# First keys' moves ahead of the small rows, the small rows on other queues, and a third score bank in the gaps of the job plan

## The reference

```python
# x: 2048 x 256; ctx_1024: 1601 x 256; E = 16 features in each of 16 heads
qh, kh, vh = heads(layernorm(x) @ Wq.T + bq), heads(ctx @ Wk.T + bk), heads(ctx @ Wv.T + bv)
scores = einsum('blhe,bshe->bhls', qh, kh) * tau + delta[:, None, None, :]
x = x + (softmax(scores / sqrt(E)) @ vh) @ Wo.T + bo
x = x + top1_expert(layernorm(x))           # 8 experts, weighted by the router's largest probability
x = x + windowed_attention(layernorm(x))    # tanh(cat @ W_c.T)
x = x + slot_mixture(layernorm(x))          # top 8 of 64 slots, GRU, slot attention, write back
```

## Time and profile before

| | us |
|---|---|
| median of 3 runs | 1069.53 (1069.47 to 1071.1) |
| the profiled execution | 1072.81, its span 1070.8 |
| PE busy / DVE busy / ACT busy in the span | 980.2 / 742.4 / 572.9 |
| maximum stage, first unit to first `pv` | 36.4 to 94.1 |
| round 0, rounds 1, 2, 3 begin at | 89.6, 249.8, 487.6, 725.6 |
| last score ends | 950.4 |

### The profile page before, as it was taken

How to read it: one execution, slowest core, us unless ns; L and a number is a source line. 1 busy time by engine, 2 the same in 40 slices (tenths; PEclk the granted TensorE clock), 3 DMA queues, 4 the chain that set the end, 5 groups by cost and what they waited for, 6 DMA issues and landing times.

```text
span 1070.8 us, 13621 instructions
## 1 busy us (share of the span) xinstructions
PE 980.2 (92%) x4794; PEld 389.6 (36%) x4794; DVE 742.4 (69%) x1704; ACT 572.9 (54%) x1063; POOL 64.5 (6%) x91
## 2 busy tenths in 40 slices
PE   7699999999899999889899989889899989889886
PEld 3353322233333334323333334323333334234643
DVE  5589888887777777767677687777677774126633
ACT  3366666666455456656455456656455466740330
POOL 3351000000000000000000000000000000100000
PEclk9899999999999999989899999999899899899899
DMA  7946500001000000001000000001000000040032
GB/s 190 190 88 112 123 1 16 16 2 35 1 16 1 15 1 11 6 1 55 1 16 1 16 1 13 4 1 55 1 16 1 1 1 21 21 127 1 1 98 79
DMA packets 34411, 36.19 MB, mean 34 GB/s; under 512 B 6766, under 2 KB 31387, under 8 KB 34083
## 3 DMA queue, kind: packets, MB, share of 16 engines
q1 hardware_dynamic: 33102, 34.43, 13.1%
q10 hardware_dynamic: 1162, 0.64, 0.4%
q0 software_dynamic: 80, 0.26, 0.1%
HBM read 21.55 MB, written 7.35 MB: 27 GB/s over the span
## 4 chain that ended last, share of the span: by engine, by line
issue 48%; PE 31%; DVE 8%; DMA 4%; SPq 3%; ACT 2%; POOL 2%; DVEq 1%; POOLq 0%; ACTq 0%
PE ps_o L1168 8%; PE ps_m L1084 8%; PE ps_e L1370 5%; DVE mx L1671 4%; DMA xres<-in_x 1%; PE ps_e L1041 1%; PE ps_m L1370 1%; SPq L558 1%; DMA q_stack<-probs 1%; PE ps_m L1188 1%; DMA d_parts<-delta_parts 1%; PE ps_m L1318 1%; POOL rstd L701 1%; POOL xres L753 1%; ACT probs L867 1%
## 5 line engine op out<-in xcount | busy, mean ns | idle before, releaser
L1671 DVE TENSOR_REDUCE mx<-ps_m 128x1 f32<-128x401 f32 x1024 | 536.1, 568 | 186.0 <-PE ps_m L1084 177.4
L867 ACT ACTIVATE probs<-ps_e 128x512 f32<-128x512 f32 (+1 forms) x763 | 438.3, 598 | 325.1 <-PE ps_e L1370 323.2
L1084 PE MATMUL ps_m<-k_stack,q_stack 99*128 99x401 bf16 x1024 | 318.6, 343 | 36.5 <-DVE mx L1671 27.0
L1370 PE MATMUL ps_e<-q_stack,k_stack 101*128 101x512 bf16 (+1 forms) x763 | 298.6, 393 | 11.2 <-ACT probs L867 9.4
L1168 PE MATMUL ps_o<-probs,v_heads 128*32 128x512 f32 (+1 forms) x1664 | 232.2, 632 | 0.0
L1370 PEld LDWEIGHTS ps_e<-q_stack,k_stack 101*128 101x128 bf16 (+1 forms) x763 | 75.5, 100 | 264.6 <-ACT probs L867 172.4
L1084 PEld LDWEIGHTS ps_m<-k_stack,q_stack 99*128 99x128 bf16 x1024 | 101.6, 99 | 183.0 <-DVE mx L1671 123.5
L1272 PE MATMUL ps_m<-expert_w,xnT 128*128 128x512 f32 x192 | 98.4, 593 | 0.7 <-DVE xb L1809 0.7
L1168 PEld LDWEIGHTS ps_o<-probs,v_heads 128*32 128x32 f32 (+1 forms) x1664 | 33.4, 109 | 62.7 <-issue 49.8
L867 ACT ACTIVATE probs<-ps_m 128x512 f32<-128x512 f32 (+1 forms) x69 | 41.5, 601 | 15.6 <-PE ps_m L1370 15.6
L1809 DVE SCALAR_TENSOR_TENSOR xb<-ps_m,hot,xb 128x256 f32<-128x256 f32 x84 | 40.6, 483 | 7.8
(11 more groups left out here) (333 smaller groups left out, 730.7 us busy)
## 6 DMA issues: line engine op xcount, KB each, us to landing
q_stack<-q_parts SPq DMA_DIRECT2D x78, 64.0 KB, 2.6
expert_w<-in_expert_wT SPq DMA_DIRECT2D x2, 1024.0 KB, 12.9
xres<-in_x SPq DMA_DIRECT2D x4, 512.0 KB, 3.8
x<-xres SPq DMA_DIRECT2D x4, 512.0 KB, 3.0
probs<-x SPq DMA_DIRECT2D x1, 2048.0 KB, 8.7
k_stack<-alphaT SPq DMA_DIRECT2D x10, 200.1 KB, 7.7
probs<-in_ctxT SPq DMA_DIRECT2D x3, 512.0 KB, 8.1
q_parts<-probs SPq DMA_DIRECT2D x4, 384.0 KB, 2.5
```

Source lines behind the costliest of these rows:

```text
L867: act.activation(probs[0:n, k % 2, h, :], score_bank(c, k, h)[0:n, :], ACT.Exp).then_inc(s["exp_done"], 1)
L1084: pe.matmul(ring_bank((n1, u))[:, 0:SPLIT], qst[0:MAX_ROW, g, h, P * t:P * t + P], kst[0:MAX_ROW, HG * g + h, QUARTER_START[q]:QUARTER_STA ...
L1370: pe.matmul(score_bank(c, k, h)[0:n, :], kst[0:ROWS, HG * g + h, P * st:P * st + n], qst[0:ROWS, g, h, :], start=True, stop=True).then_inc ...
L1671: dve.tensor_reduce(mx[:, q, col:col + 1], ring_bank((n1, u))[:, 0:SPLIT], AX.X, ALU.max)\
```

## The change

Queues first. `k_soft` is a new list of four semaphores; the last move of delta's rows, the ones and four key moves go to POOL's queue, the store of delta's parts to ACT's, and "U" leaves `START` for unit 8.

```diff
-GATHER_SP = ((0, 4, 2, 1, 5, 3), (0, 4, 2, 1), (0, 4, 2))
-GATHER_ACT = ((), (5, 3), (1, 5, 3))
+GATHER_SP = ((0, 4, 2, 1), (0, 4, 2, 1), (0, 4, 2))
+GATHER_POOL = ((5, 3), (5, 3))
+GATHER_ACT = (1, 5, 3)
...
-START = [("D",), ("L", 0), ("C",), ("K", 0, 0), ("N", 0), ("S",), ("K", 1, 0), ("T", 0), ("Q", 0, 0), ("G", 1), ("K", 2, 0), ("g",),
-         ("K", 3, 0), ("V", 0), ("V", 1), ("G", 2)]
-START += [("V", i) for i in range(2, V_EARLY)] + [("L", 1), ("U",)]
-
-BESIDE = []
+START = [("D",), ("L", 0), ("C",), ("K", 0, 0), ("N", 0), ("S",), ("K", 1, 0), ("T", 0), ("Q", 0, 0), ("K", 2, 0), ("g",),
+         ("K", 3, 0), ("V", 0), ("V", 1), ("G",)]
+START += [("V", i) for i in range(2, V_EARLY)] + [("L", 1)]
+
+BESIDE = [(8, ("U",))]
...
@@ sync
-            sp.wait_ge(s["consts_set"], 1)
-            sp.dma_start(kst[MAX_ROW:MAX_ROW + 2, 0:3 * HG, :], ones_sb[0:2, 0:S].unsqueeze(1).broadcast_to((2, 3 * HG, S)))\
-              .then_inc(s["ld_k"], 16)
-            sp.dma_start(qst[DELTA_ROW:DELTA_ROW + 3, :, :, :].rearrange("p g h t -> p g (h t)"),
-                         ones_sb[0:3, :].unsqueeze(1).broadcast_to((3, NG, HG * CT))).then_inc(s["ld_ones"], 16)
-            sp.wait_ge(s["delta_parts"], 1)
-            sp.dma_start(d_parts.rearrange("a (p s) -> p a s", s=P), delta3[:]).then_inc(s["delta_stored"], 16)
-            sp.wait_ge(s["delta_stored"], 16)
-            sp.dma_start(kst[DELTA_ROW:DELTA_ROW + 3, 0:3 * HG, :], d_parts[:, 0:S].unsqueeze(1).broadcast_to((3, 3 * HG, S)))\
-              .then_inc(s["ld_delta_k"], 16)
...
@@ gpsimd
             pool.memset(ones_sb, 1.0).then_inc(s["consts_set"], 1)
+            pool.wait_ge(s["consts_set"], 1)
+            pool.dma_start(qst[DELTA_ROW:DELTA_ROW + 3, :, :, :].rearrange("p g h t -> p g (h t)"),
+                           ones_sb[0:3, :].unsqueeze(1).broadcast_to((3, NG, HG * CT))).then_inc(s["ld_ones"], 16)
...
             pool.memset(eb[:], 0.0).then_inc(s["fills_set"], 1)
+            pool.wait_ge(s["delta_stored"], 16)
+            pool.dma_start(kst[DELTA_ROW:DELTA_ROW + 3, 0:3 * HG, :], d_parts[:, 0:S].unsqueeze(1).broadcast_to((3, 3 * HG, S)))\
+                .then_inc(s["ld_delta_k"], 16)
+            for i, rows in enumerate(GATHER_POOL):
+                first_col, end_col, last_block = KEY_PIECES[i]
+                pool.wait_ge(s["blk_parts"], BLOCK[last_block] + 1)
+                for j, row in enumerate(rows):
+                    move_k(pool, 0, (row,), k_soft[len(rows) * i + j], first_col, end_col)
             scale_shift(1)
...
                 if step[0] == "L":
                     scale_shift(step[1])
+                if step == ("L", 2):
+                    pool.dma_start(kst[MAX_ROW:MAX_ROW + 2, 0:3 * HG, :],
+                                   ones_sb[0:2, 0:S].unsqueeze(1).broadcast_to((2, 3 * HG, S))).then_inc(s["ld_k"], 16)
...
@@ scalar, step "D"
+                    act.wait_ge(s["delta_parts"], 1)
+                    act.dma_start(d_parts.rearrange("a (p s) -> p a s", s=P), delta3[:]).then_inc(s["delta_stored"], 16)
```

```diff
+def score_plan():
+    hold = {name: h for name, _, _, h in JOBS}
+    jobs = [(HG * SLOTS * (c + 1) + AT[name], name, c) for name, c in JOB if JOB[name, c][0] == 1]
+    plan, last, last_score = [], [None] * 3, {}
+    for n in range(HG * SLOTS * NC):
+        near = any(at <= n + 2 and n < at + hold[name] + 2 for at, name, _ in jobs)
+        b = min(range(2 if near else 3), key=lambda i: -1 if last[i] is None else last[i])
+        begun = [(name, c) for at, name, c in jobs if at < n]
+        plan.append((b, last[b], begun[-1] if begun else None))
+        last[b] = n
+        last_score.update({(name, c): last[2] for at, name, c in jobs if at == n})
+    return plan, last_score
...
             need(eng, bank_taken[b], n)
+            if b and LAST_SCORE[job, c] is not None:
+                eng.wait_ge(s["exp_done"], LAST_SCORE[job, c] + 1)
...
-            return ps_e[h % 2] if c else (*ps_e, ps_x)[(HG * k + h + 1) % 3]
+            return (*ps_e, ps_x)[SCORES[HG * (SLOTS * c + k) + h][0]]
...
-                        need(pe, s["exp_done"], HG * SLOTS * c + HG * k + h - (1 if c else 2))
+                        b, last, job = SCORES[HG * (SLOTS * c + k) + h]
+                        if last is not None:
+                            pe.wait_ge(s["exp_done"], last + 1)
+                        if b == 2 and job:
+                            wait_taken(pe, *job)
```

More of the change, by code:

```diff
@@ L204 @@
 RING_NO = ring_numbers()
+def score_plan():
[10 more added lines that the diff above has]
+    return plan, last_score
+SCORES, LAST_SCORE = score_plan()
 HALF_JOBS = (["ot", "y", "t1", "router", "e0", "e1", "gateT"] + [f"e{i}" for i in range(2, NE // 2)]
@@ L401, in build @@
         k_half = [sem(f"k_half{i}") for i in range(2)]
+        k_soft = [sem(f"k_soft{i}") for i in range(4)]
         q_loaded = [sem(f"q_loaded{g}") for g in range(NG)]
@@ L528, in block_cols, with wait_first_keys @@
             return k_cols[BLOCKS[b][1]][1] if BLOCKS[b][0] == "K" else CT
+        def wait_first_keys(eng, half):
+            if half == 0:
+                eng.wait_ge(k_half[0], 16 * sum(len(rows) for rows in GATHER_SP[:2]))
+                for moved in k_soft:
+                    eng.wait_ge(moved, 16)
+            else:
+                eng.wait_ge(k_half[1], 16 * K_PARTS)
         def k_loads(g):
@@ L628, in _ @@
                 sp.wait_ge(q_stored[m], 16 * NC)
-            for i, half in enumerate(k_half):
-                sp.wait_ge(half, 16 * K_PARTS * HALF_OF_PIECE.count(i))
+            for i in range(2):
+                wait_first_keys(sp, i)
             sp.wait_ge(k_loaded[1], 16 * K_PARTS)
@@ L634, in _ @@
             sp.wait_ge(s["ld_k"], 16)
+            sp.wait_ge(s["ld_ones"], 16)
             sp.wait_ge(s["ld_delta_k"], 16)
@@ L826, in step @@
                     act.activation(delta_a[:], delta_a[:], ACT.Identity, scale=E ** -0.5).then_inc(s["delta_hi"], 1)
+                    act.wait_ge(s["delta_parts"], 1)
+                    act.dma_start(d_parts.rearrange("a (p s) -> p a s", s=P), delta3[:]).then_inc(s["delta_stored"], 16)
                 if kind == "G":
-                    i = args[0]
-                    first_col, end_col, last_block = KEY_PIECES[i]
+                    first_col, end_col, last_block = KEY_PIECES[2]
                     act.wait_ge(s["blk_parts"], BLOCK[last_block] + 1)
-                    move_k(act, 0, GATHER_ACT[i], k_half[HALF_OF_PIECE[i]], first_col, end_col)
+                    move_k(act, 0, GATHER_ACT, k_half[HALF_OF_PIECE[2]], first_col, end_col)
                 if kind == "g":
@@ L1077, in max_unit @@
                     half = u // (UNITS // 2)
-                    pe.wait_ge(k_half[half], 16 * K_PARTS * HALF_OF_PIECE.count(half))
+                    wait_first_keys(pe, half)
                 if u == 0:
@@ L1145, in _ @@
                 finish()
-            pe.wait_ge(s["ld_k"], 16)
             pe.wait_ge(s["ld_delta_k"], 16)
@@ L1158, in _ @@
             pe.wait_ge(s["blk_hi"], N_BLOCKS)
+            pe.wait_ge(s["ld_k"], 16)
             def pv(c, k):
```

## The result

The changed kernel takes 1067.54 us (median of 7 runs, 1064.35 to 1068.13) against 1069.63 (7 runs, 1069.42 to 1071.1) for the kernel before beside it: ratio 0.9959, 95% interval 0.9941 to 0.9976. By the medians that is 2.1 us less, by the ratio (which is not the quotient of the two medians) 4.4, by the two profiled executions 5.0. The prediction said 12.8. The profiled execution took 1067.80, with a span of 1065.7.

A forecast was written before the change was run, and what follows sets the result against it. PE, busy 92% of the span, was taken as the bound. The start (7.9 + 2.7 - 2.2 - 0.7 = 7.7 us) and the rounds (5.1) made 12.8 off 1069.5, so 1056.7 us, range 1051 to 1063.

The forecast's parts named there:

- It is free at 14.21: Start, POOL: free behind its fill at 14.21, so its five issues at 0.96 us each end at 19.0.
- the ones for `q_stack`: Start, POOL: one issue near 3, ahead of its memsets, could cost the first projection 0 to 0.5 us; taken as 0.
- The norm's path to ACT and PE: Start: ACT's value copies end at 27.31, the first step's projection starts at 27.62; nothing in that path changes.
- The key moves themselves: Start: SP's eight out by 19.3, POOL's issues end at 19.0; first unit at 28.5 for 36.4, 7.9 us, clock 2.7 more.
- rival 2: Start: POOL's queue works off one transfer at a time, so its moves come late; 1062 us, chance 0.08.
- The rule on casts that block POOL's issues: Start: three DVE casts would each hold a POOL DMA issue, landing the last move up to 2 us later.
- "U" at unit 8: Between the units: ten mask instructions on DVE, moved from under the wait, lose 2.2 us, bounds 0.9 and 2.95.
- The ones for `k_stack`: Between the units, POOL: issued at unit 23, wanted only at the stage's end; no cost in the sum.
- The fourth chunk's load: Between the units, SP: DVE wants it 8 us earlier, key moves ahead only 4 earlier; 0.7 us lost, 0 to 3.
- The rounds: Bank plan: fewer PE waits for exp, 0.8 us in each of rounds 1 and 2, 3.5 in the last; 5.1, bounds 0 and 7.8.
- rival 3: Rounds: fewer waits mean fewer stretches at half clock, each worth up to 1.7 us; 1052 us, chance 0.14.
- Rival 4: Whole kernel slower: POOL's queue fully serial, first unit at 37.2 or later, plan gives nothing; 1074.8 us, slower or none 0.06.

The follow-up runs named there:

- all3_xb: all3 with the fourth chunk's load issued on SP ahead of the key moves of group 1; 1052.38 us, ratio 0.9824 to the kernel before.
- all3: Changed kernel with ones for `q_stack` behind POOL's first norm, masks back in `START`, ones for `k_stack` on SP; 1057.98 us, ratio 0.9876 to the kernel before.
- three single edits: Changed kernel with one edit each: `q_stack` ones behind the first norm, 1063.82 us; masks back in `START`, 1065.52; `k_stack` ones on SP, 1063.95.
- u_start: Changed kernel with one edit, the masks ("U") back ahead of the first unit instead of at unit 8; 1065.52 us, ratio 0.9937 to the kernel before.

## Why the prediction was wrong, step by step

**POOL's queue: the step that failed first.** "It is free at 14.21" and "the ones for `q_stack` cost POOL one issue near 3 ... I take 0." The row I took it from was a load followed at once by a fill (12.04, 13.01). No drain stood between them, so it couldn't tell what a drain does to a transfer in flight. The moved load stands ahead of a drain, and it also pushes back a fill that holds a cast on DVE. The price is 3.35 on POOL (11.66 less 8.31: 1.2 by the cast, some 2.2 by the drain, which ends with the load's landing), 4.1 at the first unit (33.7 to 29.6), and 6.7 at the first score with what it changed at the second fault. I had bounded it at 0 to 0.5. The norm's path to ACT and PE was one I had called unchanged.

**The key moves themselves** were right. With the drains out of the way (all3_xb) SP's eight are out by 19.35 (forecast 19.3), POOL's by 18.0 (19.0), no key move is waited for, the first unit is at 29.2 (28.5; of the 0.7, 0.3 is a later projection, 0.2 its length, and 0.2 a wait for a query move that took 6.4 to land), and the clock stays full. POOL's moves, issued between 15.04 and 17.50, landed between 23.33 and 25.68, so rival 2 did not come, though each took 8.2 to 8.6 and not the 4.6 forecast. The rule on casts that block POOL's issues, weighed as a danger, did not matter. What cost time was the other direction, POOL holding DVE, which I had not looked for.

**"U" at unit 8**: 2.2 taken, 0.9 to 2.95 as bounds; 4.9 measured in the kernel before. The upper end took each instruction at its length under the wait, where POOL ran only the norm's small operations, and PE's loss as no more than DVE's. Beside POOL's subtractions they are longer (3.8 and 5.4), and behind PE's waits of 2.9 and 4.6 the clock was at half for 3.4 and 6.8, which I had put into no term but the one removed.

**The ones for `k_stack`**: taken as free since wanted late; 2.4 measured between unit 30 and the first score. Who waits for the data was the wrong question. What mattered was the drain behind the issue.

**The fourth chunk's load**: 0.7 taken, 0 to 3. In the changed kernel it cost nothing, since DVE was late itself. Where the start ran as forecast, it cost 3.9 (all3 to all3_xb), above the upper end: it took 9.6 to land, where the longest row I had was 7.8.

**The rounds.** The size was right: 5.1 forecast, 5.4 measured in stretches of equal clock, 1.05 a round for 0.8 and 3.3 for 3.5. That it came from the waits I had counted is shown only in part: the waits for exp fell by 4.1 of 9.4, by 1.1 in each of rounds 1 and 2 and by 2.0 in the last, where 3.5 was forecast. What I counted at zero, and gave 0.14 as rival 3, came too: three pieces at half clock fewer, 4.7 us, nearly as much as the plan's own gain. Without them the two spans would lie within 1 us of each other. The forecast had no term for them, so that part of the time is luck. It is a tendency, not a fixed gain: the five kernels with the old rotation spent 47.8 to 54.6 us of rounds 1 to 3 at half clock, the eight with the plan 37.5 to 47.8, for the same instructions in the same order within each set.

**The sum**: 7.7 for the start became -4.3, 5.1 for the rounds became 10.0. The time lies above the range by the start alone. Rival 4 too had the start wrong: it let the first unit come as late as 36.3 before the start would lose, and the start lost 4.3 with the first unit at 33.7. With the three faults and the late load mended, the profile of all3_xb has 9.1 for the start and 9.3 for the rounds. Its masks are back in `START`, for which the prediction's terms give 9.9 (7.7 + 2.2).

## What to carry to other kernels

Before moving a DMA issue onto POOL's queue, look for the next drain there: here it cost until that transfer had landed, and with it all that the drain stands ahead of. Price work that is moved to DVE by what POOL does at that moment, and any wait of some microseconds by the wait and the clock after it. And when one fault is mended, look at what it had covered: here three single edits gave 6.7, 2.7 and 3.4 at the first score, together 9.6 and not 12.8, and moving the load behind them gave 3.9 more. Read a single edit's gain at several marks, since it also changes how the other faults fall.

## What the hardware showed that I had not expected

- What stood behind a drain on POOL began 0.15 to 0.3 us behind the landing of POOL's own last DMA, three times out of three (8.3, 7.4 and 4.8 us from issue to landing), and in u_start once more (62.22 and 62.42, 8.8 us).
- A cast of 13x128 on DVE took 0.22, 0.62 or 1.82 us by how long a fill on POOL ran beside it.
- Rounds with the same instructions and banks ran 37.5 to 47.8 us at half clock. What decides it no run here shows.
